# Attention keys and values loaded in pieces on SyncE's queue, two buffers for x, natural token order in the second layer

## The reference

```python
xn = layernorm(x)
s = attention0(xn)            # 16 heads of 8, clipped relative positions, softmax over all 1024 keys
g = silu(moe0(xn))            # 8 experts 128 -> 128, top 1
x = x + s * g
xn = layernorm(x)
s = attention1(xn)            # 8 heads, two softmaxes per head, causal, o = (a0 - lam * a1) v, rms norm
g = silu(moe1(xn))            # 8 experts 128 -> 256 -> 128, top 2
x = x + s * g
```

## Time and profile before

| | |
|---|---|
| median of 3 runs | 2059.43 us (2053.86 to 2059.93) |
| profiled execution, its own time | 2055.51 us |
| its span | 2053.7 us |
| token stage, layer 0 | 0 to 211.0 us, PE busy 150.7 |
| attention stage, layer 0 | 211.0 to 1188.7 us, PE busy 866.0 |
| token stage, layer 1 | 1188.7 to 1496.0 us, PE busy 284.3 |
| attention stage, layer 1 | 1496.0 to 2053.7 us, PE busy 456.6 |
| busy over the span | PE 86%, DVE 65%, ACT 58%, POOL 56% |
| DMA | 139.90 MB, 68 GB/s mean |
| ScalarE's DMA queue (q10) | 16.42 MB, nothing but key and value bursts |

### The profile page before, as it was taken

The page is one execution under the profiler, slowest core; times in us unless marked ns, Lnnn a source line. Parts: engine busy times, 40 slices in busy tenths (PEclk is TensorE's granted clock), DMA queues, the critical chain, the costliest instruction groups (busy, mean ns, idle before and its releaser), DMA issues. The chain is left out here.

```text
span 2053.7 us, 78601 instructions
## 1 busy us (share of the span) xinstructions
PE 1757.6 (86%) x34080; PEld 1323.3 (64%) x34080; DVE 1329.9 (65%) x1965; ACT 1195.0 (58%) x1438; POOL 1142.0 (56%) x1502
## 2 busy tenths in 40 slices
PE   6876699898898979989998769999969879789886
PEld 4665577777787767777877546666735545455554
DVE  5543577767677657877777334454477868777883
ACT  2322387777677757877877623444426646566555
POOL 4743479986799859997898621212012334334343
PEclk8888799999999989999999879999969989989998
DMA  3456312223221241222211121233220121211100
GB/s 99 125 155 190 107 54 60 68 68 97 71 69 49 67 121 46 63 66 64 68 45 52 61 90 53 83 86 86 69 57 23 30 63 31 48 44 28 30 23 16
DMA packets 166300, 139.90 MB, mean 68 GB/s; under 512 B 91715, under 2 KB 157014, under 8 KB 160454
## 3 DMA queue, kind: packets, MB, share of 16 engines
q1 hardware_dynamic: 153370, 105.87, 18.0%
q10 hardware_dynamic: 7212, 16.42, 3.3%
q0 software_dynamic: 5376, 12.59, 2.2%
HBM read 90.91 MB, written 43.12 MB: 65 GB/s over the span
## 5 line engine op out<-in xcount | busy, mean ns | idle before, releaser
L1348 ACT ACTIVATE a_EX<-bank 128x1024 f32<-128x1024 f32 x624 | 615.0, 1026 | 286.6 <-PE bank L1217 219.6
L1469 DVE TENSOR_TENSOR a_PM<-bank,a_PM 128x1024 f32<-128x1024 f32 x336 | 401.7, 1222 | 169.1 <-PE bank L1217 157.3
L1297 POOL TENSOR_TENSOR a_SN<-a_SN,a_MB 128x1024 f32<-128x1024 f32 x176 | 421.0, 2430 | 46.3 <-DMA a_MB<-m_dram 45.2
L1492 DVE TENSOR_REDUCE a_M<-bank 128x2 f32<-128x1024 f32 (+3 forms) x304 | 342.1, 1165 | 73.1 <-PE bank L1230 47.7
L1432 PE MATMUL bank<-a_EX,VV 128*32 128x128 f32 x9984 | 358.2, 287 | 4.5 <-issue 3.0
L1217 PE MATMUL bank<-QS,KS 51*128 51x128 bf16 (+1 forms) x4992 | 238.1, 229 | 98.1 <-DMA QS<-a_MP 48.0
L1432 PEld LDWEIGHTS bank<-a_EX,VV 128*32 128x32 f32 x9984 | 269.0, 114 | 57.2 <-issue 28.3
L1217 PEld LDWEIGHTS bank<-QS,KS 51*128 51x128 bf16 (+1 forms) x4992 | 159.2, 100 | 193.2 <-issue 59.8
L1344 ACT ACTIVATE a_SN<-bank 128x1024 f32<-128x1024 f32 x176 | 177.0, 1026 | 75.2 <-PE bank L1196 74.3
L1352 ACT ACTIVATE a_SN<-a_SN 128x1024 f32<-128x1024 f32 x176 | 185.2, 1058 | 36.6 <-POOL a_SN L1297 36.2
L1196 PE MATMUL bank<-QP,rel_t 112*128 112x32 bf16 x5632 | 198.5, 177 | 7.3 <-issue 7.0
(11 more groups left out here) (159 smaller groups left out, 2460.3 us busy)
## 6 DMA issues: line engine op xcount, KB each, us to landing
a_MB<-m_dram SPq DMA_DIRECT2D x32, 1024.0 KB, 5.0
QS<-q_dram SPq DMA_DIRECT2D x192, 96.0 KB, 3.0
KS<-k_dram ACTq DMA_DIRECT2D x12, 768.0 KB
q_dram<-t_PARTS SPq DMA_DIRECT2D x32, 192.0 KB, 2.8
k_dram<-t_PARTS SPq DMA_DIRECT2D x16, 384.0 KB, 2.9
QS<-a_MP SPq DMA_DIRECT2D x384, 2.0 KB
q_dram<-t_PARTS SPq DMA_DIRECT2D x32, 128.0 KB, 2.6
k_dram<-t_PARTS SPq DMA_DIRECT2D x16, 256.0 KB, 2.9
```

What stands on the lines that cost most here:

```text
L1297: pool.tensor_tensor(near_view(sn), near_view(sn), as_near(MB[:, :, :], it.part), ALU.add)\
L1348: act.activation(as_banks(EX[:, it.need % ER[layer]], part), by_head, ACT.Exp, scale=SCALE).then_inc(act_done, 1)
L1469: dve.tensor_tensor(pm, mb.rearrange("p hh (k i) -> p hh k i", k=4), pm, ALU.max).then_inc(max_used, 1)
L1492: dve.tensor_reduce(target.rearrange("p (hh k) -> p hh k", hh=2)[:, :, p0:p0 + g], mb[:, :, 0:g * width].rearrange("p hh (k j) -> p hh k j ...
```

## The change

- `load_kv` becomes pieces: `load_piece(layer, eng, b, k)` loads half of the keys (k = 0, 1), the values (2), both halves of the far keys (3, layer 0). SyncE issues piece k of the next batch behind the query reload of that batch's unit k. ScalarE issues no loads any more; the exponential of lambda, which stood at the start of its attention list in layer 0, stands ahead of the first output copy. Batch 0 is still loaded in one go in the token stage, by the same pieces.
- A piece from the second batch on waits for the last values product of the batch before (`room`).
- `X` and `X1` have two buffers with a semaphore each, and x is loaded one group further ahead; in layer 1 groups 0 and 1 are both loaded in the attention stage before.
- Layer 0 stores its result in natural order (the two-part store moves from layer 1 to layer 0); layer 1 works in natural order, and its mask products write each half in a row. The mask tables are made for that order.
- The planner's numbers: `kv` 3300 on ScalarE's output copy becomes 900 on SyncE's reload; `AIM`, `NEAR_BY` and `STAY` are others.

```diff
+def feeds(layer, u):
+
+    return u % NB < 4 - layer and u // NB + 1 < B
...
-        "nsub": 2560, "perm": 6480, "orms": 5700, "rows": 4000, "seen": 310, "told": 80, "rows_in": 2100, "mb_in": 5700, "q_in": 3000, "kv": 3300}
+        "nsub": 2560, "perm": 6480, "orms": 5700, "rows": 4000, "seen": 310, "told": 80, "rows_in": 2100, "mb_in": 5700, "q_in": 3000, "kv": 900}
...
-    {"perm": (0.66, -3.21), "near": (3.68, 1.21), "nmax": (-2.76, -5.89), "max": (-0.26, 0.64),
-     "maxt": (-2.51, 5.1), "mrow": (2.38, 6.43), "msplit": (-1.78, -0.53), "mb": (-1.96, -3.1),
-     "nsub": (2.05, 2.49), "nexp": (9.38, -2.88), "exp": (0.87, 0.6), "av": (5.57, 2.81), "out": (7.46, -1.4)},
-    {"max": (-0.89, 0.93), "mrow": (-5, -1.11), "msplit": (-2.16, -1.22), "exp": (1.31, 0.71),
-     "av": (4.53, -0.91), "out": (2.07, 1.41)}]
-NEAR_BY, STAY = (179, 493), (0.55, 0.47)
+    {"perm": (0.38, -3.58), "near": (3.69, 1.23), "nmax": (-2.91, -5.82), "max": (-0.26, 0.63),
+     "maxt": (-2.44, 5.62), "mrow": (1.49, 6.24), "msplit": (-1.77, -0.34), "mb": (-2.34, -3.05),
+     "nsub": (2, 2.13), "nexp": (9.88, -2.84), "exp": (0.86, 0.59), "av": (5.53, 2.81), "out": (7.63, -1.39)},
+    {"max": (-0.91, 1), "mrow": (-3.87, -0.18), "msplit": (-0.52, -1.27), "exp": (1.43, 0.71),
+     "av": (4.13, -1.01), "out": (2.3, 1.58)}]
+NEAR_BY, STAY = (236, 146), (0.59, 0.79)
...
-        done["reload", u] = add("sp", Step("reload", u), 2700 // (1 + layer), [(made, seen)], aimed="out")
+        done["reload", u] = add("sp", Step("reload", u), 2700 // (1 + layer) + (COST["kv"] if feeds(layer, u) else 0), [(made, seen)], aimed="out")
...
         elif it.kind == "reload":
             it = it._replace(need=total("exp", it.u))
+            if it.u >= NB:
+                it = it._replace(room=total("av", it.u // NB * NB - 1) + 1)
...
-        X1 = spare[:, 0:512].rearrange("p (t d) -> p t d", d=P)
-        XN1 = spare[:, 512:1536].rearrange("p (c t d) -> p c t d", c=2, d=P)
+        X1 = spare[:, 0:1024].rearrange("p (c t d) -> p c t d", c=2, d=P)
+        XN1 = spare[:, 1024:2048].rearrange("p (c t d) -> p c t d", c=2, d=P)
...
         def load_x(eng, layer, x_src, X, f):
-            eng.dma_start(X[:, :, :], x_src.rearrange("(g t p) d -> g p t d", t=GT, p=P)[f]).then_inc(x_ins[layer], 16)
+            eng.dma_start(X[:, f % 2, :, :], x_src.rearrange("(g t p) d -> g p t d", t=GT, p=P)[f]).then_inc(x_ins[layer][f % 2], 16)
...
+        def load_k(layer, eng, b, hh, far):
+            to, src = (KR, kr_dram) if far else (KS, k_dram)
+            eng.dma_start(to[hh * HALF:hh * HALF + ROWS, b % 2, :, :].rearrange("r p t -> r (p t)"),
+                          src[b][:, hh].rearrange("s d p t -> s d (p t)")).then_inc(kv_in[layer][b % 2], 16)
+
+        def load_v(layer, eng, b):
+            eng.dma_start(VV[:, b % 2, :, 0:v_dram[layer].shape[1]],
+                          v_dram[layer].rearrange("(b j p) d -> b p j d", j=NB, p=P)[b]).then_inc(kv_in[layer][b % 2], 16)
+
+        def load_piece(layer, eng, b, k):
+
+            if k < 2:
+                load_k(layer, eng, b, k, False)
+            if k == 2:
+                load_v(layer, eng, b)
+            if k == 3:
                 for hh in range(2):
...
+                    load_k(layer, eng, b, hh, True)
...
                     if layer == 0:
                         scale(pool, layer, 0)
-                    fetch_x(1)
+                    fetch_x(2)
                     scale(pool, layer, 1)
                     for f in range(GROUPS - 2):
-                        fetch_x(f + 2)
+                        if f + 3 < GROUPS:
+                            fetch_x(f + 3)
...
-                        out_h = bank[:, 2 * it.n + hh, :].rearrange("p (h c a) -> p h c a", h=4, a=2)[:, :, :, half]
+                        out_h = bank[:, 2 * it.n + hh, :].rearrange("p (h a c) -> p h a c", h=4, a=2)[:, :, half, :]
...
                             load_q(layer, sp, u + QR)
+                            if feeds(layer, u):
+                                if u >= NB:
+                                    sp.wait_ge(av_done, it.room)
+                                load_piece(layer, sp, u // NB + 1, u % NB)
...
                                 load_x(pool, 1, dst, X1, 0)
+                                load_x(pool, 1, dst, X1, 1)
...
                 def _(act):
-                    load_kv(layer, act, 1)
-                    if layer == 0:
-                        act.wait_ge(lam_sum, 1)
-                        act.activation(lam_s[:, 0:2], lam_s[:, 0:2], ACT.Exp).then_inc(lam_exp, 1)
...
                         elif kind == "ocopy":
-
+                            if layer == 0 and u == 0:
+                                act.wait_ge(lam_sum, 1)
+                                act.activation(lam_s[:, 0:2], lam_s[:, 0:2], ACT.Exp).then_inc(lam_exp, 1)
...
                             act.activation(OS[:, :], bank[:, AV, :], ACT.Copy).then_inc(o_copied, 1)
-                            if u % NB == NB - 1 and u // NB + 2 < B:
-                                load_kv(layer, act, u // NB + 2)
```

More of the change, by code:

```diff
@@ L220, in attention_tasks @@
             done["av", u, jb - ib] = value
-        done["ocopy", u] = add("act", Step("ocopy", u), COST["ocopy"] + (COST["kv"] if u % NB == NB - 1 and u // NB + 2 < B else 0), [(k, seen) for k in values] + [(last("oback", u - 1), seen)], 0, "out")
+        done["ocopy", u] = add("act", Step("ocopy", u), COST["ocopy"], [(k, seen) for k in values] + [(last("oback", u - 1), seen)], 0, "out")
         done["oback", u] = add("pe", Step("oback", u), COST["oback"], [(done["ocopy", u], told), (last("oproj", u - 1), 0)], .2, "out")
@@ L450, in build @@
         lam_exp = sem("lam_exp")
-        x_ins, x_frees, xn_readies, var_readies, rstd_readies, g_stores, proj_ins = (
+        x_ins = [[sem(f"t{layer}_x_in{i}") for i in range(2)] for layer in range(2)]
+        x_frees, xn_readies, var_readies, rstd_readies, g_stores, proj_ins = (
             [sem(f"t{layer}_{name}") for layer in range(2)]
-            for name in ("x_in", "x_free", "xn_ready", "var_ready", "rstd_ready", "g_stored", "proj_in"))
+            for name in ("x_free", "xn_ready", "var_ready", "rstd_ready", "g_stored", "proj_in"))
         perm_done = sem("perm_done")
         for k, name in enumerate("qkv"):
-            w[name, 1] = spare[:, 1536 + k * P:1536 + (k + 1) * P]
+            w[name, 1] = spare[:, 2048 + k * P:2048 + (k + 1) * P]
         lam_sum = sem("lam_sum")
@@ L505, in normalise @@
             for t in range(GT):
-                last = dve.tensor_scalar(XN[:, p, t, :], X[:, t, :], mv[:, t, 0:1], rstd[:, t:t + 1],
+                last = dve.tensor_scalar(XN[:, p, t, :], X[:, f % 2, t, :], mv[:, t, 0:1], rstd[:, t:t + 1],
                                          ALU.subtract, ALU.mult)
@@ L565, in local @@
                 return stage.enter_context(nc.sbuf_tensor(f"{n}{name}", shape, dt))
-            X = local("X", [P, GT, P]) if layer == 0 else X1
+            X = local("X", [P, 2, GT, P]) if layer == 0 else X1
             XN = local("XN", [P, 2, GT, P]) if layer == 0 else XN1
@@ L589, in token_stage @@
                 HA = local("HA", [P, GT, P])
-            x_in, x_free, xn_ready = x_ins[layer], x_frees[layer], xn_readies[layer]
+            x_free, xn_ready = x_frees[layer], xn_readies[layer]
             xt_psum, xt_ready = sem(n + "xt_psum"), sem(n + "xt_ready")
@@ L769, in _ @@
                             sp.wait_ge(v_stored, 32 + 1)
-                            load_kv(layer, sp, 0)
+                            for k in range(4 - layer):
+                                load_piece(layer, sp, 0, k)
                         elif f > 4 and f < GROUPS - 1:
@@ L1571 @@
     rel = np.asarray(L0_attn_rel_table)
-    i = HALF * (np.arange(P) % 2) + np.arange(P) // 2
     arrays = {
@@ L1575 @@
         "eye": np.eye(P, dtype=np.float32),
-        "mask": causal_tables(i),
+        "mask": causal_tables(np.arange(P)),
         "rank": np.broadcast_to((E - np.arange(E)).astype(np.float32), (P, GT, E)),
```

27 lines of the change are left out of this document (9 added, 18 removed).

## The result

The kernel after takes 2086.85 us (median of 4 runs, 2082.2 to 2096.07), the kernel before 2057.36 (4 runs, 2053.86 to 2059.93). The ratio is 1.0142, with a 95% interval of 1.0105 to 1.018. It is slower by 1.4%, where 2017 and faster was forecast. The profiled execution of after has a span (the time from its first to its last instruction) of 2087.6 us, 33.9 more than that of before. One execution of ten of a later kernel, e6_wide, took 2349.09 us at a granted clock of 0.63 in place of 0.91 to 0.92, and is left out of that kernel's ratio.

The account below looks back on a forecast made before the run. The prediction took TensorE and its waits in the two attention stages as the bound. Terms 25 + 5 + 2 - 12 - 5 + 20 + 5 = 40 us gave 2019 from the median; it said 2017, own range 2003 to 2030, 8-in-10 range 1985 to 2050.

Parts of the forecast that it names:

- it fits in front of the rows, cost 0 to 1.5 us: Layer 0 attention, SyncE's queue: a key piece is through before the maxima rows are issued, costing 0 to 1.5 us.
- rows and broadcast 2 to 5 us late: Layer 0, far-key pieces: maxima rows and broadcast come 2 to 5 us late; all layer 0 pieces entered at 12 us.
- the 7.4 us of room in rows 5: Undisturbed layer 0 unit: 7.4 us between query reload and maxima rows, the reason given for small piece costs.
- Rival 3: Slower: each key piece stands squarely in front of the rows; 2077 at 5 us a piece, 2107 at 7; chance 0.09.
- Bursts in layer 0, 25 us: Layer 0 attention: removing the load bursts that lengthen units 8 and 16 gains 25 us, at most 25.4.
- Bursts in layer 1, 5 us: Layer 1 attention: removing two bursts that delay the maxima rows gains 5 us, bounds 0 and 9.5.
- Start of attention, 2 us: Layer 0 attention start: ScalarE's DMA issue and table load leave before its first eviction; gain 2 us, bounds 1.3 and 6.3.
- Pieces in layer 1, 5 us (0 to 13): Layer 1 attention: pieces on SyncE's queue, a key piece perhaps 2 us each, cost 5 us, bounds 0 and 13.
- Mask products, 20 us: Layer 1 attention: writing mask products in a row saves TensorE 34 us, six tenths coming through: 20 us, bounds 0 and 34.
- rival 1: Layer 1: mask products do not get cheaper, or TensorE's freed time is waited away; 20 us less, 2037; chance 0.17.
- x buffers, 5 us (2 to 6): Layer 1 token stage start: with x already loaded, the query projection is taken out earlier; gain 5 us, bounds 2 and 6.
- Order of work, 0 (−18 to 18): Planner's new order across eight batches, 2.2 us each either way: 0 us, bounds -18 and +18.

Follow-up runs that it names:

- e6_wide: Kernel after with the keys laid out in DRAM so that a load has an outer dimension of 48, not 6: 2052.72 us.
- e4_behind: Kernel after with each piece issued later, behind the next unit's broadcast in layer 0 and behind its maxima rows in layer 1: 2022.97 us.
- e5_act_same: Kernel after with the pieces issued from ScalarE's queue, right behind the unit's last exponential: 2112.65 us.
- e9_behind_old: e4_behind with the planner's numbers of before, so with the old order of work: 2010.9 us.
- e3_order_x: Kernel before, bursts and order of work kept, with natural token order, two x buffers and the moved exponential of lambda: 2049.54 us.
- e1_burst: Kernel after, new order of work kept, with the loads back in one burst on ScalarE's queue: 2069.44 us.
- e2_pieces: Kernel before, old order of work kept, with only the pieces on SyncE's queue in place of the bursts: 2110.49 us.
- e12_xg_sync: Kernel after with GpSimd's two loads per unit (x and expert sums) issued by SyncE behind the output store: 2073.18 us.
- e10_nomask: e4_behind without the mask products of layer 1, so causal masking is left out there: 2024.38 us.
- e11_halfmax: e4_behind with VectorE's row maxima of layer 1 taken over half of the keys: 1992.02 us.
- e8_behind_wide: e4_behind with the keys' DRAM layout of e6_wide: 2045.87 us.
- e13_before_xg_sync: Kernel before with GpSimd's two loads per unit (x and expert sums) issued by SyncE behind the output store: 2040.31 us.
- e14_best_xg_sync: e9_behind_old with GpSimd's two loads per unit (x and expert sums) issued by SyncE behind the output store: 1996.95 us.

## Why the prediction was wrong

**The step that failed** is "it fits in front of the rows, cost 0 to 1.5 us", and with it "rows and broadcast 2 to 5 us late" for the far keys. Three things in it were misread.

First, the 7.4 us of room in rows 5, for which the prediction kept its small figures, run from the start of the reload to the rows. The piece goes behind the reload's end (629.44), from where it is 4.8 us. And this was not a unit that gets a piece: over the twelve that do, the room in before is 0.8 to 4.8 us, 2.8 on average.

Second, the rows are not what stands behind the piece. The maxima store does, some 0.1 us behind the reload in all twelve, and the broadcast waits for its landing. The prediction listed it among what stands behind and then priced the pieces by the rows. Measured, as lateness of the broadcast: 3.6 us for a key piece and 6.1 for the far keys against before, 5.5 and 7.3 against the same order of work with the pieces out of the way. Layer 0 is 45.2 us shorter in e4_behind, where 12 stood (bounds 0 and 20). The prediction's own figures for a batch, two key pieces, far keys and values, add up to 2.5 to 8.5 us and not to 0 to 7, which is too small a slip to matter here.

Third, the prediction concluded from a rule that beside a piece, on another queue, the rows would be let through. e5_act_same has the store as late beside a piece on another queue; at most the maxima rows were let through there, and the kernel got slower. The Trainium skill (DMA: Bandwidth & Descriptors, section Queues, rings and completion order) says that each DMA engine takes turns between the queues that it has work for; it does not say that a small transfer is then on time, and here it was not.

Rival 3, slower, had the place and the sign: it decided from 3.8 us a piece and gave 2077 at 5 us. It had a chance of 0.09, since the room of 7.4 us spoke against it. That its number lies near 2087 is partly luck: it stood on 57 us of gains, 20 of them for the masks, which did not come, and it charged nothing for far keys.

**The other terms:**
- *Bursts in layer 0, 25 us:* about right. e9_behind_old against e3_order_x, same order, burst gone and pieces out of the way: 899.7 to 875.0, 24.7 us. That it is so close is luck: in the new order the same step (e1_burst to e4_behind) shows 14.2 us, and over both layers the medians fell by 38.6 us in the old order and 46.5 in the new one, where 30 stood.
- *Bursts in layer 1, 5 us:* 1.7 us in the same pair (503.6 to 501.9), although TensorE's waits for rows fell from 31.7 to 10.7. Its waits for the maxima did not rise; its busy time for the same work did, from 413.5 to 425.9 us between the two copies. In the new order the step shows 18.9 us (521.9 to 503.0).
- *Start of attention, 2 us:* the first output copy came 3.4 us earlier, and TensorE no longer waits for the first eviction. But this does not show the loads' part: e1_burst and e3_order_x still issue them there and have the copy at 279.84 and 281.48, as early as after, and e2_pieces does not and has it at 286.71, later than before. Measured from the stage's first product, the copy comes after 73.5 to 78.2 us in the four kernels with the exponential of lambda at the stage's start, and after 69.2 to 71.9 in those that moved it, e6_wide (75.5) aside. That makes the exponential the likelier cause; it was not tested alone.
- *Pieces in layer 1, 5 us (0 to 13):* after against e4_behind 19.7. In the old order the pieces stand in front of the rows, as the prediction had it, but at 8.6 us and not 2 (e2_pieces). In the new order GpSimd's drain comes into it, which the prediction did not have: e12_xg_sync, without GpSimd's loads, is 13.8 us shorter there.
- *Mask products, 20 us:* the cause was right and the gain was not. They became cheaper, 417 to 281 ns each, 29.0 us in all:

```profile
L1224 PE MATMUL bank<-mask_b 64*128 64x256 bf16 x512 | 51.7, 281 | 0.0
```

  but e3_order_x has layer 1 only 4.5 us shorter, and e10_nomask shows that even their absence is worth nothing. "Six tenths come through" was the step that failed here; rival 1 had it.
- *x buffers, 5 us (2 to 6):* 8.2 us (347.0 to 338.8). The other kernels with one buffer have 343.9 to 344.5 us there, those with two 336.5 to 339.5 (e11_halfmax aside), so 4 to 8 us are nearer to it. The query projection was taken out 2.1 us after it started (1217.22 to 1219.33), not 7.7. In layer 0 the wait moved into the next one, as said: VectorE waits 20.27 us for the value store, not 14.57.
- *Order of work, 0 (−18 to 18):* costs 5 to 20 us, and most where rows are late.

Run by run, the 30.1 us of layer 0 are +3.0 for token order and x (before to e3_order_x), −24.7 for the bursts (to e9_behind_old), +6.6 for the order of work (to e4_behind) and +45.2 for the place of the pieces (to after). The 14.6 us of layer 1 are −4.5, −1.7, +1.1 and +19.7 in the same steps. Such a chain adds up by construction; it is no proof of its parts, and 3.0 and 6.6 lie within the 14 us that single stages scatter.

**Left open:** why e8_behind_wide is slower than e4_behind; whether e12_xg_sync, e13_before_xg_sync and e14_best_xg_sync gain by the drain or by the issue time that GpSimd saves; and how much of the loss is the granted clock, which fell in the attention of layer 1 from 0.94 to 0.88 between before and after and rose to 0.95 in e14_best_xg_sync.

## What to carry to other kernels

Splitting a burst helps only if every piece has a place with nothing needed behind it: look at the very next DMA of the queue, and at who waits for its landing, in each unit that gets a piece and not in a sample one. Another queue did not protect it (2113 us); a place behind the last urgent transfer did (2087 to 2023 us). And a cheaper operation on the busiest engine can be worth nothing where another engine's chain holds it back, whatever the busy shares say: find out by leaving each of the two out.

## What the runs showed of the hardware

- A drain on GpSimd stood for 10.05 us behind GpSimd's own two loads of 64 KB while a key load was under way, and the profile puts it under "issue". At this place it was 45.3 us in layer 1 of after, and 0.4 us once SyncE issued these loads (e12_xg_sync).
- A store of 8 KB reached the point where its broadcast could be issued after 11.3 us behind a load of 768 KB on the same queue, after 10.9 us beside one from another queue (e5_act_same), and after 5.7 us with the load out of the way (e4_behind).
- In the 4 us behind the start of a load of 768 KB, other traffic included, the DMA share was 0.53 at 128 GB/s with an outer dimension of 6, and 1.04 at 213 GB/s with one of 48 and the same bytes (e6_wide).
- Matrix products into every second float of a PSUM bank took 417 ns for 256 columns, in a row 281. The Trainium skill (SBUF — State Buffer, section Door 1: The DMA port swizzle) says that any non-contiguous access to PSUM slows matrix products; the trace agrees.
- TensorE with 51.7 us less to do in layer 1 was busy only 7.8 us less (448.77 to 440.94, e4_behind and e10_nomask): the mean granted clock of the stage was 0.83 in place of 0.87, between the levels of 1.2 and 2.4 GHz. So most of the removed work came back as slower work.
